# Projection with stationary weights on column halves, turned back by transposes, and three small changes around it

## What is computed

```
x = x + conv_attention(group_norm(x))          # 8 heads of 32, windows of 8x8, plus a 3x3 convolution of v
t = t + axial_attention(layer_norm(t))         # one 32x32 table of scores per head over the batch, summed over 256 positions
        #  o = einsum('sth,tlhc->slhc', att, v) * sigmoid(mn @ Wg + bg);  o @ Wo + bo     (256 -> 64)
t = t + mixture(layer_norm(t))                 # router (64 -> 8), best 2 of 8 experts,
        #  w2 @ (silu(w1 @ x) * (w3 @ x)), hidden size 682, weighted by the two gates
```

## Time and profile before

| | us |
|---|---|
| median of 3 runs | 868.36 (866.83 to 872.11) |
| the profiled execution, its own time | 872.92 |
| its span | 870.7 |
| PE busy | 775.1 (89%) |
| DVE busy | 617.6 (71%) |
| ACT busy | 430.0 (49%) |
| POOL busy | 393.9 (45%) |

### The profile page before, as it was taken

The page is one execution under the profiler, slowest core; times in us unless marked ns, Lnnn a source line. Parts: engine busy times, 40 slices in busy tenths (PEclk is TensorE's granted clock), DMA queues, the critical chain, the costliest instruction groups (busy, mean ns, idle before and its releaser), DMA issues.

```text
span 870.7 us, 22770 instructions
## 1 busy us (share of the span) xinstructions
PE 775.1 (89%) x8182; PEld 484.1 (56%) x8182; DVE 617.6 (71%) x1522; ACT 430.0 (49%) x828; POOL 393.9 (45%) x450
## 2 busy tenths in 40 slices
PE   4789999999987899699988788889999999999970
PEld 3757777777765566387776633233444443434450
DVE  6568989898874676438879757777666667676754
ACT  2536666666662344345534254554545454545540
POOL 1044555545541111004777773777744444444550
PEclk9969999999995999899989889899999999999995
DMA  6027301111008960000004112222232323222109
GB/s 217 1 44 115 56 12 24 26 27 27 3 2 267 338 201 3 2 2 15 28 28 73 31 40 37 52 50 52 52 54 39 52 40 50 44 48 36 26 7 289
DMA packets 182358, 54.64 MB, mean 63 GB/s; under 512 B 157472, under 2 KB 176897, under 8 KB 182000
## 3 DMA queue, kind: packets, MB, share of 16 engines
q1 hardware_dynamic: 168688, 43.44, 23.8%
q0 software_dynamic: 8704, 8.54, 3.0%
q10 hardware_dynamic: 4864, 1.31, 0.7%
HBM read 25.19 MB, written 28.51 MB: 62 GB/s over the span
## 4 chain that ended last, share of the span: by engine, by line
PE 42%; DVE 10%; issue 3%; ACT 2%; DMA 1%; ACTq 0%; POOL 0%; SPq 0%; DVEq 0%; POOLq 0%
PE bank L1344 19%; PE bank L1365 10%; PE bank L1282 2%; PE bank L1377 2%; PE bank L1352 2%; PE bank L1369 2%; PE bank L1273 1%; PE bank L1255 1%; PE bank L1264 1%; PE bank L1291 1%; DVE av_og L1514 1%; DVE norm_T L1765 1%; ACT norm_T L1472 1%; DVE residual L1785 1%; DVE norm_T L1783 1%
## 5 line engine op out<-in xcount | busy, mean ns | idle before, releaser
L1765 DVE TENSOR_TENSOR norm_T<-norm_T,bank 128x512 f32<-128x512 f32 (+7 forms) x234 | 136.6, 591 | 100.1 <-ACT norm_T L1472 96.0
L1236 POOL DMA_INDIRECT chosen_out<-ex_out,ex_id x144 | 142.6, 990 | 126.3 <-DVE norm_T L1765 63.9
L1344 PE MATMUL bank<-ex_xt,ex_w 64*128 64x512 f32 (+7 forms) x780 | 183.4, 590 | 17.5 <-DVE norm_T L1765 7.3
L1227 POOL DMA_INDIRECT slot_x<-rows,slots x128 | 124.3, 971 | 86.6 <-issue 70.6
L1472 ACT ACTIVATE norm_T<-bank 128x512 f32<-128x512 f32 (+7 forms) x234 | 122.4, 526 | 82.7 <-PE bank L1344 78.3
L1344 PEld LDWEIGHTS bank<-ex_xt,ex_w 64*128 64x128 f32 x780 | 71.1, 189 | 98.8 <-issue 63.3
L1365 PE MATMUL bank<-norm_T,ex_w 128*64 128x512 f32 (+7 forms) x390 | 102.1, 576 | 0.8 <-ACT ex_w L1459 0.8
L451 POOL TENSOR_TENSOR probs<-shifted,win_rden 128x512 f32<-128x512 f32 x64 | 66.7, 1043 | 14.5 <-DVE win_rden L623 8.5
L1365 PEld LDWEIGHTS bank<-norm_T,ex_w 128*64 128x64 f32 x390 | 29.7, 139 | 69.1 <-issue 64.2
L1465 ACT ACTIVATE norm_T<-bank 128x512 f32<-128x512 f32 (+7 forms) x39 | 21.8, 559 | 80.8 <-PE bank L1369 80.8
L443 POOL TENSOR_TENSOR xp<-norm_T,one_of_each 128x256 fp32r<-128x256 f32 x32 | 19.7, 615 | 83.9 <-PE ps_c L512 83.7
(11 more groups left out here) (266 smaller groups left out, 1471.0 us busy)
## 6 DMA issues: line engine op xcount, KB each, us to landing
slot_x<-blank SPq DMA_DIRECT2D x1, 17028.0 KB, 56.4
ex_x<-slot_x SPq DMA_DIRECT2D x128, 64.0 KB
norm_T<-chosen_out SPq DMA_DIRECT2D x8, 512.0 KB, 7.1
w_rows<-in_L_ffn_w_dram SPq DMA_DIRECT2D x32, 84.0 KB
wlocal_in<-in_L_conv_w_local_dram SPq DMA_DIRECT2D x6, 384.0 KB, 9.9
chosen_out<-ex_out,ex_id POOLq DMA_INDIRECT x144, 2.2
residual<-in_x_dram SPq DMA_DIRECT2D x2, 1024.0 KB, 7.0
residual<-in_x_dram SPq DMA_DIRECT2D x4, 512.0 KB, 7.4
```

The source lines that it names most:

```text
L1227: eng.indirect_dma_start(s.slot_x[:, :], bass.IndirectOffsetOnAxis(slot[:, k, tile:tile + 1], 0), rows[m % RING][:, k, t, :], None).then_i ...
L1236: eng.indirect_dma_start(s.chosen_out[:, :], bass.IndirectOffsetOnAxis(ex_id[k % OUTS][some, j:j + 1].bitcast(U32), 0), out[k % OUTS][some ...
L1344: eng.matmul(ps[b][:, 0:width(k)], w13[par][halves(i), c * HCHUNK:(c + 1) * HCHUNK], xt[par][halves(i), 0:width(k)], start=True, stop=True ...
L1765: eng.tensor_tensor(h[par][:, c, columns(c, k)], act[c % DEEP][:, columns(c, k)], ps_3[c % deep3(k)][:, columns(c, k)], ALU.mult).then_inc ...
```

## The change

- `conv_attention`, `scores`: the two-column product with the identity is left out.
- `axial_scores`: z holds each token's 64 channels twice, written by one DVE instruction of 1024 elements per partition, and `turn_x` becomes four transposes of 128x128. DVE's copy `right_side(2m-1, 1)` moves behind the Newton steps and z.
- `dispatch_and_experts`: the projection keeps the weights stationary, one half of the 256 inputs for each half of the output partitions; ACT copies the result; PE transposes it back in four transposes, in the middle of the next attend; DVE adds the two halves in two instructions. The turn of centred tokens is four transposes. Ranks and counts come from two products in place of three.

```diff
@@ scores
-                    eng.matmul(ps_s[0][0:D, 0:2], s.ident[:, 0:D], s.ident[:, 0:2], start=True, stop=True)
@@ axial_scores
-        z = [tmp(f"ax_z{i}", [P, PAIR, C]) for i in range(2)]
+        z = [tmp(f"ax_z{i}", [P, PAIR, 2, C]) for i in range(2)]
@@ turn_x
-                        for i in range(2):
-                            last = eng.matmul(ps_x[halves(i), t * P:(t + 1) * P], z[j // 2 % 2][:, j % 2 * GROUP + t, :], s.ident[:, :],
-                                              start=True, stop=True)
+                        last = eng.transpose(ps_x[:, t * P:(t + 1) * P], z[j // 2 % 2][:, j % 2 * GROUP + t].rearrange("p i c -> p (i c)"), s.ident[:, :])
@@ DVE's loop
-                    if m >= 1:
-                        right_side(2 * m - 1, 1)
                     if m < PAIRS:
                         newton_norm(eng, mine, b, root_n, m + 1)
...
-                        eng.tensor_tensor(z[m % 2][:, :, :], b.xc[:, :, :], b.rstd[:, :].unsqueeze(2).to_broadcast(wide), ALU.mult).then_inc(z_n, 1)
+                        twofold = [P, PAIR, 2, C]
+                        eng.tensor_tensor(z[m % 2][:, :, :, :], b.xc[:, :, :].unsqueeze(2).to_broadcast(twofold),
+                                          b.rstd[:, :].unsqueeze(2).unsqueeze(3).to_broadcast(twofold), ALU.mult).then_inc(z_n, 1)
                     if m >= 1:
+                        right_side(2 * m - 1, 1)
                         right_side(2 * m - 1, 3)
@@ dispatch_and_experts, tensor
-                def attend(g):
+                def attend(g, m):
...
                 def project(g):
                     eng.wait_ge(og_n, 2 * g + 2)
                     wait(eng, res_n, g)
+                    for m in range(2):
+                        last = eng.matmul(ps_r[halves(m), :], s.wo[:, m, :], og[g % 2][:, m, :], start=True, stop=True)
+                    last.then_inc(c_n, 1)
+
+                def turn_back(g):
+                    eng.wait_ge(cc_n, g + 1)
                     for t in range(GROUP):
-                        for m in range(2):
-                            last = eng.matmul(ps_r[:, t * C:(t + 1) * C], og[g % 2][:, m, t * P:(t + 1) * P], s.wo[:, m, :],
-                                              start=(m == 0), stop=(m == 1))
+                        last = eng.transpose(ps_r[:, t * P:(t + 1) * P], across[:, t * P:(t + 1) * P], s.ident[:, :])
                     last.then_inc(r_n, 1)
@@ turn
-                    for t in range(PAIR):
-                        pair, i = divmod(t, 2)
-                        last = eng.matmul(home_of_x(m)[halves(i), pair * P:(pair + 1) * P], xc[m % 2][:, t, :], s.ident[:, :],
-                                          start=True, stop=True)
+                    for pair in range(GROUP):
+                        last = eng.transpose(home_of_x(m)[:, pair * P:(pair + 1) * P], xc[m % 2][:, 2 * pair:2 * pair + 2, :].rearrange("p t c -> p (t c)"),
+                                             s.ident[:, :])
@@ ranks
-                    eng.matmul(places, lower[:, :], chosen[:, :, 1:PAIR + 1].rearrange(by_token), start=True, stop=False)
-                    eng.matmul(places, ones[:, :], ahead[:, :, 0:PAIR].rearrange(by_token), start=False, stop=True)
-                    eng.matmul(ps_q[:, COUNTS], ones[:, :], ahead[:, :, PAIR], start=True, stop=True).then_inc(ranked_n, 1)
+                    places = ps_q[:, RANKS.start:COUNTS.stop].rearrange("p (t e) -> p t e", e=EXPERTS)
+                    eng.matmul(places, ones[:, :], ahead[:, :, :].rearrange(by_token), start=True, stop=True)
+                    eng.matmul(places[:, 0:PAIR, :], lower[:, :], chosen[:, :, 1:PAIR + 1].rearrange(by_token), start=False, stop=True,
+                               skip_group_check=True).then_inc(ranked_n, 1)
@@ PE's loop over g, after project(g - 1) and ranks
-                        attend(g)
+                        attend(g, 0)
+                    if 1 <= g <= GROUPS:
+                        turn_back(g - 1)
+                    if g < GROUPS:
+                        attend(g, 1)
@@ scalar: new, called after the gates of step g and before exp
+                def copy_across(g):
+                    eng.wait_ge(c_n, g + 1)
+                    eng.activation(across[:, :], ps_r[:, :], ACT.Copy).then_inc(cc_n, 1)
@@ vector, residual
-                    eng.tensor_tensor(t, t, ps_r[:, 0:GROUP * C].rearrange("p (t c) -> p t c", c=C), ALU.add).then_inc(res_n, 1)
+                    both = ps_r[:, :].rearrange("p (t m c) -> p t m c", m=2, c=C)
+                    mine.then(eng.tensor_tensor(t, t, both[:, :, 0, :], ALU.add))
+                    eng.tensor_tensor(t, t, both[:, :, 1, :], ALU.add).then_inc(res_n, 1)
```

More of the change, by code:

```diff
@@ L1018, in dispatch_and_experts @@
         og = [tmp(f"av_og{i}", [P, 2, GTOK]) for i in range(2)]
+        across = tmp("av_across", [P, GTOK])
         rows = [tmp(f"rows{i}", [P, 2, PAIR, ROW]) for i in range(RING)]
@@ L1065, in dispatch_and_experts @@
         LOGITS, RANKS, COUNTS = slice(0, 64), slice(64, 128), slice(128, 136)
-        v_n, va_n, g_n, gc_n, o_n, og_n, r_n, res_n = (
-            sem(f"av_{n}") for n in ("v", "v_copied", "gates", "gates_copied", "o", "gated", "projected", "residual"))
+        v_n, va_n, g_n, gc_n, o_n, og_n, c_n, cc_n, r_n, res_n = (
+            sem(f"av_{n}") for n in ("v", "v_copied", "gates", "gates_copied", "o", "gated", "projected", "across_copied", "turned_back", "residual"))
         center_n, sq_n, rstd_n, z_n, x_n, xt_n, l_n, below_n, exp_n, picked_n, ranked_n, slots_n, rows_n, tab_n = (
@@ L1264, in gates @@
                         eng.matmul(ps_g[m][:, :], s.wg[halves(m), :], s.xt[halves(m), g * GTOK:(g + 1) * GTOK], start=True, stop=True).then_inc(g_n, 1)
-                def attend(g):
-                    eng.wait_ge(va_n, 2 * g + 2)
-                    for m in range(2):
-                        wait(eng, og_n, 2 * g - 1 + m)
-                        for t in range(GROUP):
-                            for i in range(4):
-                                hd = 4 * m + i
-                                last = eng.matmul(ps_o[m][i * D:(i + 1) * D, t * P:(t + 1) * P], v[g % 2][:, t, hd * D:(hd + 1) * D],
-                                                  s.att_w[:, place(hd), :], start=True, stop=True)
-                        last.then_inc(o_n, 1)
+                def attend(g, m):
+                    if m == 0:
+                        eng.wait_ge(va_n, 2 * g + 2)
+                    wait(eng, og_n, 2 * g - 1 + m)
+                    for t in range(GROUP):
+                        for i in range(4):
+                            hd = 4 * m + i
+                            last = eng.matmul(ps_o[m][i * D:(i + 1) * D, t * P:(t + 1) * P], v[g % 2][:, t, hd * D:(hd + 1) * D],
+                                              s.att_w[:, place(hd), :], start=True, stop=True)
+                    last.then_inc(o_n, 1)
                 def project(g):
@@ L1299, in ranks @@
                     by_token = "p e t -> p t e"
-                    places = ps_q[:, RANKS].rearrange("p (t e) -> p t e", e=EXPERTS)
-                    eng.matmul(places, lower[:, :], chosen[:, :, 1:PAIR + 1].rearrange(by_token), start=True, stop=False)
-                    eng.matmul(places, ones[:, :], ahead[:, :, 0:PAIR].rearrange(by_token), start=False, stop=True)
-                    eng.matmul(ps_q[:, COUNTS], ones[:, :], ahead[:, :, PAIR], start=True, stop=True).then_inc(ranked_n, 1)
+                    places = ps_q[:, RANKS.start:COUNTS.stop].rearrange("p (t e) -> p t e", e=EXPERTS)
+                    eng.matmul(places, ones[:, :], ahead[:, :, :].rearrange(by_token), start=True, stop=True)
+                    eng.matmul(places[:, 0:PAIR, :], lower[:, :], chosen[:, :, 1:PAIR + 1].rearrange(by_token), start=False, stop=True,
+                               skip_group_check=True).then_inc(ranked_n, 1)
                 def logits(m):
@@ L1403, in _ @@
                 ranks(PAST - 1)
+                turn_back(GROUPS - 1)
                 eng.wait_ge(va_n, 2 * GROUPS)
@@ L1445, in _ @@
                             eng.activation(gate[g % 2][:, m, :], ps_g[m][:, :], ACT.Tanh, bias=s.bg[:, m:m + 1], scale=0.5).then_inc(gc_n, 1)
+                    if 1 <= g <= GROUPS:
+                        copy_across(g - 1)
                     m = chunk(g, 4)
@@ L1453, in _ @@
                         across_x(m)
+                copy_across(GROUPS - 1)
                 def weights(k, par):
```

## The result

The changed kernel takes 876.03 us, median of 9 runs (874.76 to 877.6), against 871.89 us of the kernel before on the same chip, 9 runs (866.81 to 874.45): a ratio of 1.0065 of the means (4.1 us by the medians), 95% interval 1.0039 to 1.0091. The forecast was 870.5 with a range of 857 to 883, and 2.1 us more than before. The sign and the size of the routing loss came out as worked out; two smaller things were not foreseen, a gain that the axial stage did not keep and a loss in the experts' stage, of whose instructions the change touches only one set of ranks.

The account below looks back on a forecast made before the run. PE was taken to bound convolution and mostly axial scores, a loop through PE and DVE routing. Terms -4.6 - 5.5 + 12.4 - 0.2 = +2.1 us on 872.92 gave 875.0; run medians being 4.6 lower, 870.5, range 857 to 883.

Parts of the forecast that it names:

- Convolution, -4.6: Convolution stage: leaving out the small product saves 0.15 us for each of 32 images; 4.6 us taken, bounds 0 and 4.9.
- my small allowance for DVE: Convolution: DVE may take over in some images, so 4.6 us was taken of the 4.9 in all.
- Axial scores, -5.5: Axial stage: shorter turns save 4.8 us over the pairs, the last wait for z 0.7; bounds 3.5 and 6.5.
- 0.64 a pair, times 7.5 pairs: Axial scores: each pair saves 0.52 us in its first half and 0.12 in its second, 4.8 in all.
- so z is not later: Axial scores: z, at most double its 0.69 us, comes no later, since DVE no longer makes a copy before the Newton steps.
- Routing, PE leg +0.28: Routing cycle, from turn of centred tokens to DVE's residual: 6.52 us against 6.24, 0.28 more.
- DVE leg +1.40: Routing cycle, from DVE's residual to the next turn: 10.16 us against 8.76, with a new wait of 0.50.
- Experts, -0.2: Experts' stage: its ranks, made with fewer products, give back 0.2 us; the stage's other parts are not touched.
- (b): Routing: PE is the bound after all and DVE's small work slides into freed time; 7.9 us off, 850; chance 0.17.
- (c): Plain routing cycles: PE's waits lower its clock to 1.2 GHz, 3.4 us more in each of five, 887; chance 0.15.
- (d): Convolution: the small product was needed, so nothing is gained or the first load stalls as long; 875; chance 0.13.
- (e): Routing: the change costs half of the forecast loss; 864; chance 0.10.

Follow-up runs that it names:

- numbers 2: Kernel before with only the axial scores' change (z written twice, four transposes, DVE's copy moved): 868.70 us, ratio 0.9962 to the kernel before.
- number 3: Kernel before with only the new projection, ACT's copy, turn back and two residual instructions; old turn and ranks: 887.74 us, ratio 1.0192 to the kernel before.
- number 6: Changed kernel with a second, unread copy of the same size on ACT ahead of the real one: 878.20 us, ratio 1.0070 to the kernel before.
- Experiment 8: Kernel before with the 17 MB slot fill moved from the axial stage to the end of the convolution's weight loads: 869.25 us, ratio 0.9964.
- number 4: Changed kernel with the projection put back as it was before: 859.43 us, ratio 0.9859 to the kernel before.
- 9: Changed kernel with the old projection and the slot fill moved to the end of the convolution's weight loads: 854.06 us, ratio 0.9788 to the kernel before.
- number 1: Kernel before with only the small identity product taken out: 864.47 us, ratio 0.9920 to the kernel before.
- 7: Changed kernel with one of DVE's two residual instructions left out, so tokens and routing differ: 867.11 us, ratio 0.9949 to the kernel before.
- number 5: Changed kernel with the turn back moved right behind the projection, ahead of ranks and attend: 869.75 us, ratio 0.9975 to the kernel before.
- 10: Changed kernel with old projection, early slot fill, and ACT's fill of the rows behind exponential, square and logits copy: 854.52 us, ratio 0.9791 to the kernel before.

## Why the prediction was right, and what it had wrong

**Convolution, -4.6:** 0.153 an image (6.383 to 6.230), 4.8 us over the stage: nothing took over, against my small allowance for DVE. DVE's slack shrank by the same 0.15: in the odd image that followed a turn of rows its first maximum starts 0.10 behind the end of that turn, where the earlier trace rows show a wait of 0.25 (timeline of DVE):

```profile
150.32 0.59 DVE L631 STREAM_TRANSPOSE w_sb<-w_rows 128x448 f32<-128x448 f32 x1
151.01 0.69 DVE L608 TENSOR_REDUCE win_max<-ps_s 128x8 f32<-128x512 f32 x1
```

The ledger has 5.8; the kernel's first half-clock stretch was shorter (6.8 + 3.4 us against 17.1). The runs do not tie this to the change: numbers 2 and 3, which still have the small product, have 6.8 + 3.4 as well, and number 6, without it, has 17.1.

**Axial scores, -5.5: the step mis-sized.** The price of a pair was right, 0.63 for 0.64, and so was the wait for z, 0.9 for 0.7. The stage gave 3.3. The step that failed is "0.64 a pair, times 7.5 pairs": I had read one clean pair and the sum took all of them to be clean, when two of five already had stops in the trace before. With the pair shorter the stops cost 4.70 in place of 3.07, and this 1.6 accounts for most of the missing 2.2. Experiment 8 shows that they go with the fill. Why they cost more beside the shorter pairs is not shown. Another 0.5 is the step "so z is not later": it holds in the clean pairs and at the stage's end, but in the stage's head z is 1.23 us long in place of 0.69 and PE's wait is 2.46 in place of 1.93. The sum had put the head at nothing.

**Routing, PE leg +0.28:** 415.80 - 409.31 = 6.49 against 6.24, so +0.25. **DVE leg +1.40:** 426.08 - 415.80 = 10.28 against 8.76, so +1.52. The 0.12 is mostly in the ranks, which take 422.00 - 421.34 = 0.66 where I had 0.55. Waits 2.07, 0.49 and 1.40 for 1.9, 0.5 and 1.5. Cycles of 16.73, 16.72, 16.77, 16.75 and 16.65 for 16.68. The stage cost 1.0 + 10.4 = 11.4 for 12.4; what is less lies in the cycles around the tables: before, 15.52 and 15.27 were already longer than 15.00, and the second table's cycle took only 0.9 more. One wording in the prices is wrong and changes no number: the "sixteen products" that turned the tiles are eight products of two instructions each, in the axial stage four tiles twice over.

**Experts, -0.2:** +1.7, not foreseen. Of that stage's instructions only one set of ranks changed (two products in place of three, at 527 us), the term of -0.2, too small to be seen here. The length from first to last tile was between 338.2 and 341.1 us in all the kernels here. The stretches of the two kernels, same window, before and then after, columns as in rows 1:

```profile
495.00:525.00 30.00, 22.71 (x118) 10.99 (x117) 19.02 (x58) 12.90 (x20) 22.88 (x24) 0.83 0.16 35
```

```profile
495.00:525.00 30.00, 23.53 (x82) 9.43 (x84) 18.50 (x57) 11.42 (x17) 18.20 (x19) 0.66 0.14 31
```

A mean granted clock of 0.66 and not 0.83 around the stage's start goes with the loss. The twelve traces say more than one window, which lies at different tiles in different kernels. From the 20th tile to the last all twelve kernels take 149.2 us, and all but 0.1 of the difference arises between the first and the tenth, 100.5 to 103.4 us. It goes with the time that the clock was at its 1.2 GHz level between first and last tile: 11.4 to 11.9 us in numbers 3, 4 and 9, whose stage took 338.2 to 338.5; 17.1 to 17.8 in the kernel before and numbers 1, 2, 7 and 8, with 339.3 to 339.8; 23.0 and 23.1 in number 5 and the changed kernel, with 341.0 and 341.1. Numbers 6 (15.8 us, 338.2) and 10 (14.3 us, 339.3) lie between and in the wrong order. This is an association over the kernels run, not an experiment. It stays open what sets the clock at the stage's start, and whether the change has a part in it.

**The rivals.** (b) PE as the bound: refuted by cycles of 16.7 and, from the other side, by number 5, in which PE stands more and the cycle is shorter. (c) the clock: it was at the 2.4 GHz level through the first four plain cycles but for 0.15 us, with three waits of 0.78 to 1.40 in the one shown; it fell in the last 6.7 us of the fifth, which was none the longer for it. The stretch at the lower level over the end of the stage is 13.6 us in the changed kernel and in numbers 3 and 6, which have the longest cycles, and 3.4 to 10.3 in the other nine, so the rival may have a part in the 1.7 us of the experts' stage. In number 3 a plain cycle did fall, for 3.4 us, and that cycle was 1.2 longer; twice that, 2.4, for the 6 to 7 us that the rival named is less than its 3.4. The Trainium skill, TensorE: Matmul & The Clock Gate, Part 4, says that transposes do not count as PE activity in the same way; cycles with twelve transposes each at a granted clock of 1.00 do not speak for a cost of that here. Four transposes take 409.90 - 409.31 = 0.59 in the timeline, the form switch with them. The same part's figure of about 275 ns, stated for one of 128x128 in bf16, fits the trace as the length of one: the records of single transposes in the changed kernel last 273 ns in the median, but they start 110 ns apart and overlap. As a distance it would make 1.1 for four, and there the measurement decides. (d) refuted by number 1. (e) half of the cost in routing: refuted, 11.4 of 12.4 in the profiled executions.

So the whole came out 1.5 us above the forecast by difference (+3.6 in the profiled executions against +2.1), and by the runs, 0.65% or 5.7 us, 3.6 above. That it came so near is in part luck: against the terms of the sum the axial stage lost 2.1 and the experts' stage 1.9, and the convolution with 1.2, routing with 1.0 and the end with 0.3 took most of it back. The time itself is 5.5 above the 870.5, since the kernel before is at 871.89 here and not at the 868.36 that the forecast started from. The projection itself costs 17 us by experiment 3's ratio to the kernel before and 18 by the step from number 4 to the changed kernel, and all the rest of the change gives 12 back (number 4).

## What to carry to other kernels

When two engines share a loop, count what an edit does to the time at which the partner gets its result, not the busy time it saves: here the projection's own PE time fell from 1.93 to 1.01 us, and the loop grew by 1.7 a cycle because the result went through one more copy, stood behind half an attend, and was read by two instructions instead of one. Before a per-iteration saving is multiplied, list the distances of all the iterations: those that are not clean say what else is running there, and in this kernel moving that transfer alone was worth as much as the axial change alone (0.9964 and 0.9962). After a good edit look at the next queue that is late (ACT's fill of the rows here); it was worth 0.2 to 0.4 us in three of the five plain cycles, and nothing that the total could tell.

## What the runs showed of the hardware that I had not expected

- PE stops of 0.4 to 2.6 us in the middle of a run of like matrix products, for which the profile shows no releaser, beside a fill that moved 300 to 340 GB/s; the same fill beside the convolution stage caused none. In a stretch of 14 us with two of them the kinds of transfers include four packets of the kind "instruction". That these came late behind the fill's is my guess for the cause; nothing here shows it.
- In number 4 such a stop of 1.65 was followed by 3.4 us at a lower granted clock, and that pair took 14.38; in the changed kernel the same stop of 1.65 was not followed by one, and the pair took 12.75.
- Two copies of 128x512 on ACT, each shown as 0.59 to 0.60, start 0.47 to 0.50 apart: the second costs the loop less than its row says (cycles +0.37 in number 6).
